# Two mask granules in one byte plane, all mask bytes in SBUF, the joining of planes and layer 1's normalised rows on GpSimd

## The reference

```python
def layer0(h, adj, a):
    e = (h @ a[:64])[:, None] + (h @ a[64:])[None, :]
    e = where(e > 0, e, 0.01 * e)
    att = softmax(where(adj > 0, e, NEG_INF), axis=1)
    return att @ h
def layer1(x, adj, w, a, bias):        # the same on wh = x @ w, plus bias
    ...
x = layernorm(x + layer0(x, adj, a0))
x = layernorm(x + layer1(x, adj, w1, a1, bias1))
```

## Time and profile before

| | us |
|---|---|
| median of three runs | 505.31 (504.54 to 505.81) |
| profiled execution, its own time | 506.67 |
| its span, first to last instruction | 504.7 |
| PE busy | 445.2 |
| DVE busy | 410.1 |
| ACT busy | 388.0 |
| GpSimd busy | 85.0 |

### The profile page before, as it was taken

How to read it: one execution, slowest core, us unless ns; L and a number is a source line. 1 busy time by engine, 2 the same in 40 slices (tenths; PEclk the granted TensorE clock), 3 DMA queues, 4 the chain that set the end, 5 groups by cost and what they waited for, 6 DMA issues and landing times.

```text
span 504.7 us, 11767 instructions
## 1 busy us (share of the span) xinstructions
PE 445.2 (88%) x4420; PEld 416.0 (82%) x4420; DVE 410.1 (81%) x736; ACT 388.0 (77%) x587; POOL 85.0 (17%) x60
## 2 busy tenths in 40 slices
PE   0799768888989799797988989999999999999991
PEld 0489757877979698797978968999999999999991
DVE  3789999889899898988988989794868595958655
ACT  2694178878988978987893928899999999999800
POOL 0011221514215151331514020010101010101010
PEclk9978879997989999897999957999999999999998
DMA  7999999999999999999983100202030302113000
GB/s 187 252 239 263 262 261 289 331 295 322 320 315 330 298 338 305 306 314 301 326 249 127 44 0 7 79 2 95 3 94 0 94 13 81 55 38 93 2 13 10
DMA packets 80294, 87.71 MB, mean 174 GB/s; under 512 B 7298, under 2 KB 76162, under 8 KB 80258
## 3 DMA queue, kind: packets, MB, share of 16 engines
q1 hardware_dynamic: 45602, 52.98, 37.0%
q10 hardware_dynamic: 34656, 34.21, 24.7%
HBM read 77.74 MB, written 9.44 MB: 173 GB/s over the span
## 4 chain that ended last, share of the span: by engine, by line
PE 46%; DMA 20%; DVE 20%; issue 11%; SPq 1%; ACT 1%; POOL 0%; DVEq 0%; ACTq 0%; POOLq 0%
PE acc L418 39%; DMA stage<-in_adj 17%; DVE narrow L784 4%; DVE turned L796 4%; DMA xn<-in_x 3%; DVE pos L810 2%; PE misc L371 2%; PE srow L320 1%; DVE num L854 1%; PE flip L351 1%; DVE num L847 1%; DVE red L840 1%; SPq L225 1%; PE misc L401 1%; DVE bn L859 1%
## 5 line engine op out<-in xcount | busy, mean ns | idle before, releaser
L557 ACT ACTIVATE neg<-srow,dcol 128x512 int8 (+1 forms) x512 | 354.2, 855 | 19.3 <-issue 9.8
L418 PE MATMUL acc<-xy_old,pos 128*128 128x195 bf16 x1024 | 194.7, 260 | 24.2 <-POOL pos L988 18.4
L418 PE MATMUL acc<-xy_old,neg 128*128 128x195 bf16 x1024 | 194.4, 260 | 0.0
L418 PE MATMUL acc<-stage,pos 128*128 128x195 bf16 x1024 | 178.8, 248 | 0.0
L418 PE MATMUL acc<-stage,neg 128*128 128x195 bf16 x1024 | 178.6, 249 | 0.0
L418 PEld LDWEIGHTS acc<-xy_old,pos 128*128 128x128 fp8e4 x1024 | 105.9, 103 | 32.8 <-issue 31.4
L418 PEld LDWEIGHTS acc<-xy_old,neg 128*128 128x128 fp8e4 x1024 | 105.4, 103 | 1.3
L418 PEld LDWEIGHTS acc<-stage,pos 128*128 128x128 fp8e4 x1024 | 101.0, 99 | 4.7 <-issue 4.5
L418 PEld LDWEIGHTS acc<-stage,neg 128*128 128x128 fp8e4 x1024 | 100.5, 98 | 0.4 <-issue 0.3
L784 DVE TENSOR_SCALAR narrow<-stage 128x4096 uint8<-128x4096 int32 x32 | 75.0, 2344 | 16.4 <-DMA stage<-in_adj 15.5
L975 POOL TENSOR_TENSOR small<-small,minus_half 128x4 f32<-128x4 f32 x16 | 35.1, 2193 | 214.4 <-DVE small L862 214.4
(11 more groups left out here) (117 smaller groups left out, 311.6 us busy)
## 6 DMA issues: line engine op xcount, KB each, us to landing
stage<-in_adj ACTq DMA_DIRECT2D x64, 512.0 KB, 9.0
stage<-in_adj SPq DMA_DIRECT2D x64, 512.0 KB, 9.1
spill<-turned SPq DMA_DIRECT2D x16, 512.0 KB, 7.7
turned<-spill SPq DMA_DIRECT2D x16, 512.0 KB, 3.7
out<-x1s SPq DMA_DIRECT2D x8, 128.0 KB, 1.9
xn<-in_x SPq DMA_DIRECT2D x1, 768.0 KB, 16.9
kept<-in_x SPq DMA_DIRECT2D x4, 128.0 KB, 3.9
kept<-in_x ACTq DMA_DIRECT2D x4, 128.0 KB, 4.9
```

What stands on the lines that cost most here:

```text
L418: last = nc.tensor.matmul(acc[:, r, c * XW:(c + 1) * XW], masks[c][:, t // BYTES, t % BYTES, r * P:(r + 1) * P], xy[layer][:, g * GT + t, ...
L557: last = nc.scalar.activation(o[:, t // BYTES, t % BYTES, :], srow[:, bass.ds((s % 2) * 512, 512)], ACT.Sign, bias=dcol[:, layer, col:col ...
```

## The change

Granules 2p and 2p+1 become a pair. `to_bytes` writes the even one as 0 or 0x38 into `narrow` and the odd one as 0 or 0x40 (2.0 in fp8) into `narrow_odd`. GpSimd adds the two byte planes as 1024 words a partition (`join`), and one `turn` a pair moves the result into `kept`, which now holds all masks. `spill`, `turned` and the reloads go. `mask` takes a granule's bits out of the shared plane with its code: two DVE instructions of 1024 words in both layers, which read the plane and `neg`; GpSimd's half of `pos` goes. The tables of odd granules are halved in `split`, since their mask is worth 2.0. Layer 1's input (layer 0's output) is normalised by GpSimd in four instructions instead of by ACT, and GpSimd's product with minus the mean goes, with DVE's instruction for it. ACT issues a granule's loads ahead of its signs. The DVE order in the prologue and in `body0` is new.

```diff
-    KEEP = NG // 2
+    PAIRS = NG // 2
-    CODE = 0x38
-    CODES = 0x38383838
+    CODE = (0x38, 0x40)
+    CODES = (0x38383838, 0x40404040)
+    WORTH = (1.0, 2.0)
...
         def mask_at(s, g):
-            if g < KEEP:
-                return kept[:, bass.ds(s * (KEEP * GN) + g * GN, GN)]
-            return turned[:, g - KEEP, :]
+            return kept[:, bass.ds(s * (PAIRS * GN) + g // 2 * GN, GN)]
...
             def body0(s, first=False):
-                for g in range(1, NG):
+                for g in range(NG):
                     if g == NG - 1 and not first:
                         copy_x1(s - 1)
+                    load_next(s + 1, g)
                     signs(0, s + 1, g)
-                    load_next(s + 1, g)
...
-                step(nc.vector.tensor_tensor(rest, wh[layer][:, t, :].unsqueeze(1).broadcast_to(shape),
-                                             wts[:, :, t].unsqueeze(3).broadcast_to(shape), ALU.mult))
+                if g % 2:
+                    for c in range(2):
+                        last = nc.vector.scalar_tensor_tensor(rest[:, c], wh[layer][:, t, :], 1.0 / WORTH[1],
+                                                              wts[:, c, t].unsqueeze(2).broadcast_to((P, GT, E)),
+                                                              ALU.mult, ALU.mult)
+                    step(last)
+                else:
+                    step(nc.vector.tensor_tensor(rest, rows, weights, ALU.mult))
...
-            def turn(s, g):
-
-                k = s * NG + g
-                if g >= KEEP and s > 0:
-                    dve.wait_ge(pos_ready, k - NG + 1)
-                    dve.wait_ge(spilled[g - KEEP], 16 * s)
-                dve.wait_ge(narrowed, k + 1)
-                nc.vector.transpose(words(mask_at(s, g)), words(narrow[:, 0:GN])).then_inc(turned_ready, 1)
+            def turn(s, pair):
+
+                dve.wait_ge(joined, s * PAIRS + pair + 1)
+                nc.vector.transpose(words(mask_at(s, 2 * pair)), words(narrow[:, 0:GN])).then_inc(turned_ready, 1)
...
-                if layer == 0:
-                    half = slice(GW // 2, GW)
-                    nc.vector.scalar_tensor_tensor(words(pos[:, g, :])[:, half], c[:, half], CODES, a[:, half],
-                                                   ALU.bitwise_xor, ALU.bitwise_and).then_inc(pos_half, 1)
-                    dve.wait_ge(pos_half, k + 1)
-                nc.vector.tensor_tensor(c, c, a, ALU.bitwise_and).then_inc(neg_ready, 1)
-                if layer == 1:
-                    dve.wait_ge(neg_ready, k + 1)
-                    nc.vector.tensor_tensor(words(pos[:, g, :]), a, c, ALU.bitwise_xor).then_inc(pos_ready, 1)
+                nc.vector.scalar_tensor_tensor(c, a, CODES[g % 2], c, ALU.bitwise_and, ALU.bitwise_and)\
+                  .then_inc(neg_ready, 1)
+                dve.wait_ge(neg_ready, k + 1)
+                nc.vector.scalar_tensor_tensor(words(pos[:, g, :]), a, CODES[g % 2], c,
+                                               ALU.bitwise_and, ALU.bitwise_xor).then_inc(pos_ready, 1)
...
+            def body0(s, first=False):
+
+                to_bytes(s + 1, 0)
+                if not first:
+                    residual_sum(0, s - 1)
+                mask(0, s, 2)
+                if not first:
+                    moments(0, s - 1)
+
+                to_bytes(s + 1, 1)
+                mask(0, s, 3)
+                turn(s + 1, 0)
+
+                to_bytes(s + 1, 2)
+                mask(0, s + 1, 0)
+                if s == NS - 2:
+                    far_columns(0)
+                read_acc(0, s)
+
+                to_bytes(s + 1, 3)
+                average(0, s)
+                if s == NS - 2:
+                    column_max(0)
+                mask(0, s + 1, 1)
+                if first:
+                    source_vectors()
+                turn(s + 1, 1)
...
+            def normalize(s):
+
+                pool.wait_ge(std_ready, s + 1)
                 pool.sem_inc(pool_turn, 1)
-                nc.gpsimd.tensor_tensor(shift_n, minus_mean, rstd, ALU.mult).then_inc(std_ready, 1)
-
-            def positive(s, g):
-
-                pool.wait_ge(neg_ready, s * NG + g + 1)
+                for r in range(RB):
+                    last = nc.gpsimd.tensor_scalar(xn[:, row_at(s, r), :].rearrange("p o d -> p (o d)"), y[:, r, :],
+                                                   mv[:, r, 0:1], rstd[:, r:r + 1], ALU.subtract, ALU.mult)
+                last.then_inc(x1_ready, 1)
+
+            def join(s, pair):
+
+                pool.wait_ge(narrowed, s * NG + 2 * pair + 2)
                 pool.sem_inc(pool_turn, 1)
-                half = slice(0, GW // 2)
-                nc.gpsimd.tensor_tensor(pos[:, g, :].bitcast(U32)[:, half], mask_at(s, g).bitcast(U32)[:, half],
-                                        neg[:, g, :].bitcast(U32)[:, half], ALU.subtract).then_inc(pos_ready, 1)
...
+            for s in range(2):
+                for pair in range(PAIRS):
+                    join(s, pair)
+            for s in range(2, NS):
+                inverse_std(0, s - 2)
+                join(s, 0)
+                normalize(s - 2)
+                join(s, 1)
```

More of the change, by code:

```diff
@@ L82, in sem @@
             return ctx.enter_context(nc.semaphore(name))
[L84 to L86 removed]
+        kept = sb("kept", [P, NS * PAIRS * GN], U8)
         stage = sb("stage", [P, SLOTS, GR * JC], I32)
         narrow = sb("narrow", [P, 2 * GT * E * 4], U8)
[L89 removed]
+        narrow_odd = sb("narrow_odd", [P, GN], U8)
         neg = sb("neg", [P, RING, GN], U8)
@@ L180, in gat_kernel @@
         turned_ready = sem("turned_ready")
-        spilled = [sem(f"spilled{g}") for g in range(NG - KEEP)]
-        reloaded = [sem(f"reloaded{g}") for g in range(NG - KEEP)]
+        joined = sem("joined")
         signs_ready = sem("signs_ready")
         neg_ready = sem("neg_ready")
-        pos_half = sem("pos_half")
         pos_ready = sem("pos_ready")
@@ L449, in body0 @@
                     project(s - 1)
-                granule(0, s + 1, 1)
                 if last:
@@ L454, in body0 @@
                     spread_max(0)
+                granule(0, s + 1, 1)
                 granule(0, s + 1, 2)
@@ L560, in signs @@
                     last.then_inc(signs_ready, 1)
-            def normalize(s):
-                act.wait_ge(std_ready, 2 * s + 2)
-                act.sem_inc(act_turn, 1)
-                for r in range(RB):
-                    last = nc.scalar.activation(xn[:, row_at(s, r), :].rearrange("p o d -> p (o d)"), y[:, r, :],
-                                                ACT.Identity, bias=shift_n[:, r:r + 1], scale=rstd[:, r:r + 1])
-                last.then_inc(x1_ready, 1)
             def copy_x1(s):
@@ L608, in _ @@
                 body0(s)
-            for g in range(1, NG):
+            for g in range(NG):
                 if g == NG - 1:
                     copy_x1(NS - 3)
-                signs(0, NS - 1, g)
                 if g + SLOTS < NG:
                     load_next(NS - 1, g)
+                signs(0, NS - 1, g)
             copy_wh(NS - 3)
-            normalize(NS - 2)
             act.wait_ge(shift_ready, 3)
@@ L624, in _ @@
             copy_wh(NS - 2)
-            normalize(NS - 1)
             copy_x1(NS - 1)
@@ L905, in _ @@
             to_bytes(0, 0)
+            tables0(1)
+            to_bytes(0, 1)
+            tables0(2)
             turn(0, 0)
+            to_bytes(0, 2)
             mask(0, 0, 0)
-            for g in range(1, NG):
-                to_bytes(0, g)
-                turn(0, g)
-                tables0(g)
-                if g < NG - 1:
-                    mask(0, 0, g)
+            tables0(3)
+            mask(0, 0, 1)
+            to_bytes(0, 3)
             row_factors0()
@@ L916, in _ @@
                 dve.wait_ge(s_x[n], 16)
-            for s in range(NS - 1):
+            turn(0, 1)
+            body0(0, first=True)
+            for s in range(1, NS - 1):
                 body0(s)
+            residual_sum(0, NS - 2)
+            mask(0, NS - 1, 2)
+            moments(0, NS - 2)
             near_shift()
-            mask(0, NS - 1, NG - 1)
+            mask(0, NS - 1, 3)
             dve.wait_ge(exp_ready, 5)
@@ L926, in _ @@
             moments(0, NS - 1)
+            mask(1, 0, 0)
             near_tables(1)
-            mask(1, 0, 0)
             mask(1, 0, 1)
@@ L970, in _, with words @@
         def _(pool):
+            pool.sem_inc(x1_ready, 1)
+            def words(ap):
+                return ap.bitcast(U32)
             def inverse_std(layer, s):
```

95 lines of the change are left out of this document (19 added, 76 removed).

## The result

The changed kernel takes 525.91 us (median of four runs, 524.33 to 526.16). The kernel before took 505.56 in the same comparison (504.54 to 508.52). The ratio is 1.038, interval 1.034 to 1.042: slower by about 20 us. The forecast was 520, and its range 496 to 526.

What follows compares the result with a forecast made beforehand. Layer 0 was taken as paced by DVE, with DMA close behind. Bodies +14.0, start -2.3 and end +2.9 gave +14.6 on 505.3, or 520 us; range 496 to 526.

Steps and rivals of the forecast that it cites:

- rival 1: Layer 0's bodies: GpSimd's joins run beside DVE, bodies -9.8 us, time 496 us, faster; chance 0.20.
- Rival 3: Layer 0's bodies: one join hidden, the other costs 2.25 (504 us), or 1.1 and the whole (512 us); chance 0.15.
- Turns, -16.4: DVE in layer 0's seven bodies: two of four turns a body go, 14 x 1.17 = -16.4 us.
- masks, +15.1: DVE in layer 0's bodies: 28 masks, each two 1024-word instructions, 2.40 instead of 1.86 us, +15.1 us.
- Joins, +31.5: Layer 0's bodies: two GpSimd joins a body each delay DVE by 2.25 us, 14 x 2.25 = +31.5 us.
- My lower row: GpSimd's 4-element product, 0.85 us, gave a lower join estimate of 1.70; set aside as having waited, 2.4 taken.
- Waits for adj, -13.7: DVE in layer 0's bodies: without the spill, 8.4 MB at 319 GB/s take 26.3 us; all 13.7 us of waits go.
- DMA's share well under 1: Sign expected in the changed profile, with no waits for adj and a body of 32 us.
- rival 2: Layer 0's bodies: like rival 1, but DMA takes over at 282 GB/s, 29.8 us a body, 503 us; chance 0.10.
- Start, -2.3: Layer 0's prologue: turns, masks, waits and joins sum to -2.3 us; the first body starts near 60.
- Between the layers, +2.9: Behind layer 0's last body: two masks on DVE instead of one, 2.40 + 0.54 = +2.9 us.
- 1 us early as PE starts with less backlog: Between the layers: PE's last normalised rows can be 2 us late or 1 us early; taken at 0.

Runs made afterwards that it cites:

- the run with memsets: The changed kernel with each join replaced by two GpSimd memsets of the same 1024 words, the second waiting for the first: 512.07 us, ratio 1.011.

## Why the prediction was right, term by term

The mechanism was the one forecast, and rival 1 (joins beside DVE) is refuted by the rows of the changed kernel and by the experiment without joins. Rival 3 (one of the two joins hidden) is refuted by the same rows: both joins hold. The size is less good than the verdict. The measured 525.9 lies 0.1 below the upper end of the range, and 6 above the forecast. In the bodies the forecast was +14.0 and the trace has +13.4, but this agreement is partly luck: it hides three errors that nearly cancel (-2.5, +3.6, -2.1). What is missing lies between the layers.

- **Turns, -16.4, and masks, +15.1.** Two turns a body go, and a mask that isn't held takes 1.25 + 1.15 us. Both as forecast. The mask step by itself, in the kernel before, moved the time by only 5 us, since waits for adj took up the rest.
- **Joins, +31.5.** Forecast 2.25 each, measured 2.07 on both held instructions, or 14 x 2.07 = 29.0. Right in kind and place, the second mask instruction and the average's second product, and 2.5 too large. My lower row (the product of 4 elements, 0.85) was rightly set aside: where no DVE instruction holds it, it takes 0.20.
- **Waits for adj, -13.7.** In the changed kernel 3.6 us are left, all of them in its first two bodies (3.0 and 0.6). This step was mis-sized. I took DMA's pace from the body at 319 GB/s, where the spill was a part of it, and let the smaller amount run at that rate. The runs give 273 to 297 GB/s for adj alone in bodies that wait for it. So the sign "DMA's share well under 1" didn't come either: it was 0.98 to 0.99 in the bodies from the third to the sixth. Had the joins cost nothing, this term would have been wrong by 15 us, and 0.20 for rival 1 against 0.10 for rival 2 was the wrong way round.
- **Moved work.** The last body's residual and moments now come behind it, 2.1 us that the first body saves. The forecast left this out of both sums. It makes the bodies' terms fit: -16.4 + 15.1 - 1.0 - 10.1 - 1.5 + 29.0 - 2.1 = +13.0, for 13.4 measured.
- **Start, -2.3.** Measured -2.0. The prediction's own terms add up to -2.1, not -2.3. (Another slip of it: PE has 35.1 us more busy time than DVE, not 34. Nothing rests on it.) In the prologue the first join held a cast, 2.75 us for 0.70, and DVE waited 1.9 us for PE.
- **Between the layers, +2.9.** Measured +7.5, and on another path than the sum had it. The forecast added DVE's masks, and the moved work (2.1 us) lies on DVE there too. But the chain that ended last runs over PE. Before the last body has ended PE begins with three granules instead of two, and DVE's PSUM reads wait for it, 3.5 us in four waits; before, they waited for nothing. The stretch in windows (columns as above), and the first of DVE's waits:

```profile
284.20:288.70 4.50, 4.50 (x29) 4.11 (x30) 4.43 (x10) 0.00 (x0) 0.00 (x0) 0.50 0.01 4
288.70:303.10 14.40, 14.40 (x168) 14.40 (x166) 10.50 (x21) 8.76 (x14) 6.65 (x5) 1.00 0.00 1
```
```profile
299.06 0.56 DVE L778 TENSOR_REDUCE red<-acc 128x130 f32<-128x390 f32 x1 [1.15 <-PE acc L389]
```

The three granules take 18.96 us where two took 11.19, 7.8 more. One granule at full clock is 5.6 of that. The other 2.2 come with the granted clock: it was 0.50 (1.2 GHz) up to 288.7, PE having stood idle for 2.1 us just before 284.16, and 1.00 (2.4 GHz) for both granules in the kernel before. From there to the transpose of the last rows it is 12.6 us instead of 11.7, of which PE waits 2.5 for GpSimd's rows. Behind it 1.0 us is won back, and 0.15 at the head of this stretch. The prediction had booked "1 us early as PE starts with less backlog"; it starts with more. This is the term that was missing, 4.6 us.

The spans differ by 18.9 us and the forecast was 14.6. Of the 4.3 missing, +4.6 lie between the layers, +0.3 at the start and -0.6 in the bodies.

The Trainium skill's rule ("SBUF — State Buffer", "Who interferes with whom") said that a DVE instruction with two SBUF inputs contends with a GpSimd instruction that reads SBUF, and that the first holds the other for its whole length. The traces now show both directions: 3.29 for 1.22 us on DVE, and 3.43 for 2.40 on GpSimd, where the other engine's instruction had started first. They also agree with the same section that a GpSimd instruction which only writes doesn't hold such an instruction (1.23 us beside a memset). By the estimate from the Trainium skill ("GPSIMD Engine Reference", "Performance versus the Vector engine") the join was 2.3 us; it took 2.39 beside PSUM reads.

## What to carry to other kernels

Work handed to GpSimd isn't free for DVE: if it reads SBUF, it costs DVE nearly its own length wherever a DVE instruction with two operands starts behind it, and DVE doing it itself may be cheaper (here 1.25 us against 2.07). Look for instructions whose duration doesn't fit their form, since such holds are counted as busy. And where a load queue is nearly full, taking traffic away or cutting the consumer's work pays only in part: take the pace of what stays from several stretches in which it runs alone. And where an engine's work moves behind the end of a stage, look at which engine has the backlog there: the added work may be hidden, and the backlog not.

## What was not expected of the hardware

- Four GpSimd tensor_scalar instructions of 128x64 took 4.7 to 6.3 us in the changed kernel, against 1.44 for ACT's four. Most of that is DVE in the way: in the first such group of the run with memsets, beside a transpose and then an idle DVE, they take 0.62 each:

```profile
L953 POOL TENSOR_SCALAR xn<-num,mv,small 128x64 f32<-128x64 f32 x4 | 2.4, 619 | 0.0
```

- adj alone, in rows of 1 KB, came at 273 to 294 GB/s a body in the kernel without joins and at 288 to 297 in the kernel before without the spill, with DMA's share at 1.06 to 1.11. With the spill beside it DMA moved 310 to 319 in all in the second to sixth body, at a share of 1.07 to 1.10 (one of them in the earlier trace rows). So the share doesn't tell how near the rate is to its best.
- A join also holds a 4-element tensor_scalar of DVE (1.53 us for 0.17) and a cast (2.75 for 0.70), and a memset holds the tensor_scalar (1.03). bn_stats and PSUM reads pass a join, and a transpose passes GpSimd's half of `pos` (1.24 us at 162.79, with GpSimd from 163.13).
